# Layer 1's attention: DVE adds two of a head's four pair-sum tiles, and TensorE makes three products with ones a head instead of four

## The reference, cut to what matters

```python
q, k, v = (qkv[:, :, i].transpose(0, 2, 1, 3) for i in range(3))
attn = softmax(einsum('bhqd,bhkd->bhqk', q, k) * hd ** (-0.5), axis=-1)
o = einsum('bhqk,bhkd->bhqd', attn, v).transpose(0, 2, 1, 3).reshape(B, T, D)
```

## Time and profile before

| | |
|---|---|
| Time, median of 3 runs | 3868.43 us (3863.33 to 3868.81) |
| The profiled execution's own time | 3865.6 us |
| Its span | 3863.7 us |
| PE busy | 3588.0 us, 93% of the span |
| DVE busy | 2666.8 us, 69% |
| ACT busy | 2306.9 us, 60% |
| POOL busy | 1921.6 us, 50% |
| Mean granted clock of TensorE | 0.968 |

### The profile page before, as it was taken

The page is one execution under the profiler, slowest core; times in us unless marked ns, Lnnn a source line. Parts: engine busy times, 40 slices in busy tenths (PEclk is TensorE's granted clock), DMA queues, the critical chain, the costliest instruction groups (busy, mean ns, idle before and its releaser), DMA issues. The chain is left out here.

```text
span 3863.7 us, 68702 instructions
## 1 busy us (share of the span) xinstructions
PE 3588.0 (93%) x25924; PEld 2519.3 (65%) x25924; DVE 2666.8 (69%) x4271; ACT 2306.9 (60%) x4011; POOL 1921.6 (50%) x2187
## 2 busy tenths in 40 slices
PE   8997999999999989899999986889999999995999
PEld 7885777767777767777778863446666666652555
DVE  4335888888888866667753327867777777755987
ACT  2225888888888855333333326745555555554988
POOL 1003555555555533444444436646666666663554
PEclk9998999999999999999999998979999999997999
DMA  5546333333323139334431116853334333314221
GB/s 187 186 162 164 64 70 64 70 64 69 62 59 64 40 131 338 104 107 155 148 104 44 50 55 234 313 106 73 64 76 81 66 70 79 74 32 137 83 77 50
DMA packets 284776, 403.16 MB, mean 104 GB/s; under 512 B 89704, under 2 KB 146540, under 8 KB 283930
## 3 DMA queue, kind: packets, MB, share of 16 engines
q1 hardware_dynamic: 284448, 398.78, 37.3%
HBM read 248.95 MB, written 148.93 MB: 103 GB/s over the span
## 5 line engine op out<-in xcount | busy, mean ns | idle before, releaser
L634 POOL TENSOR_SCALAR biastile<-dist,ascale 128x1024 f32<-128x1024 f32 x512 | 574.9, 1123 | 489.4 <-DVE mn L588 476.2
L796 ACT ACTIVATE PT<-st 128x512 f32<-128x512 f32 x1024 | 544.9, 606 | 419.1 <-PE st L730 415.3
L810 DVE TENSOR_REDUCE mn<-s 128x1 f32<-128x1024 f32 x512 | 596.4, 1216 | 273.7 <-PE s L720 273.7
L873 POOL TENSOR_TENSOR two<-PT 128x1024 f32<-128x1024 f32 x256 | 603.5, 2377 | 305.0 <-ACT PT L796 304.9
L588 DVE CUSTOM_DVE_ANT_0 Sn<-sp,biastile 128x1024 f32<-128x1024 f32 x512 | 621.9, 1215 | 78.5 <-PE pt L521 46.7
L559 ACT ACTIVATE Sn<-Sn,mn 128x1024 f32<-128x1024 f32 x512 | 586.9, 1146 | 18.9 <-DVE mn L588 18.8
L521 PEld LDWEIGHTS pt<-ident,Sn 128*128 128x128 f32 x4096 | 454.9, 141 | 177.5 <-issue 150.9
L521 PE MATMUL pt<-ident,Sn 128*128 128x128 f32 x4096 | 546.9, 277 | 22.1 <-DVE og L601 22.1
L549 ACT ACTIVATE PT<-pt 128x512 f32<-128x512 f32 x576 | 337.6, 598 | 136.3 <-PE pt L521 126.3
L730 PE MATMUL st<-QS,KS 98*128 98x512 f32 x1024 | 376.4, 425 | 1.3 <-ACT PT L796 1.2
L720 PE MATMUL s<-KS,QS 96*128 96x512 f32 x1024 | 353.7, 428 | 25.3 <-DMA KS<-s_khi 23.6
(11 more groups left out here) (257 smaller groups left out, 6503.2 us busy)
## 6 DMA issues: line engine op xcount, KB each, us to landing
QS<-s_qhi SPq DMA_DIRECT2D x128, 256.0 KB, 5.1
KS<-s_khi SPq DMA_DIRECT2D x128, 256.0 KB, 6.9
KS<-s_klo SPq DMA_DIRECT2D x64, 256.0 KB, 6.2
QS<-s_qlo SPq DMA_DIRECT2D x64, 256.0 KB, 6.8
Vp<-s_v SPq DMA_DIRECT2D x64, 256.0 KB, 7.7
s_o<-og SPq DMA_DIRECT2D x32, 512.0 KB, 4.0
xA<-in_x SPq DMA_DIRECT2D x8, 1024.0 KB, 5.9
s_qhi<-qstage SPq DMA_DIRECT2D x32, 256.0 KB, 2.0
```

The costliest lines, as they stand in the source:

```text
L634: nc.gpsimd.tensor_scalar(bt[s % 2][:], dist[:, t, :], K.ascale[:, n % H:n % H + 1], 1.0, ALU.mult, ALU.mult).then_inc(*s_bias.up())
L796: nc.scalar.activation(pT[n % 2][:, kb, g * BLK:(g + 1) * BLK], pst_r.at["st", u, g][:], ACT.Exp, scale=-1.0).then_inc(*s_exp.up())
L810: nc.vector.tensor_reduce(mn[n % 2][:, t:t + 1], ps_r.at[u][:], AX.X, ALU.min).then_inc(*s_min.up())
L873: nc.gpsimd.tensor_tensor(two[m % 6][:], pT[n % 2][:, 2 * k, :], pT[n % 2][:, 2 * k + 1, :], ALU.add).then_inc(*s_two.up())
```

## The change

DVE adds the first two pair sums of a head, k = 0 and k = 1, in place into the buffer of k = 1. It does so in step 2n + 6, after the four minima and the copy `mr`, and signals `s_four`. `total(n)` now waits once for all four pair sums, makes the products of k = 2 and k = 3, waits for `s_four`, and makes the product of the tile that DVE has added. It signals `s_sum` once a head instead of four times, and the waits on it count heads.

```diff
+        def add_four(n):
+            m = n * LT // 2
+            dve.wait_ge(s_two, m + 2)
+            nc.vector.tensor_tensor(two[(m + 1) % 6][:], two[m % 6][:], two[(m + 1) % 6][:], ALU.add).then_inc(*s_four.up())
```

```diff
-        def total(m):
-            n, k = divmod(m, LT // 2)
-            pe.wait_ge(s_two, m + 1)
-            for g in range(4):
-                op = nc.tensor.matmul(po[g * HD:(g + 1) * HD, QW:2 * QW], K.ones[:, 0:HD], two[m % 6][:, g * QW:(g + 1) * QW],
-                                      start=k == 0, stop=k == LT // 2 - 1)
+        def total(n):
+            pe.wait_ge(s_two, (n + 1) * LT // 2)
+            for k in (2, 3, 1):
+                if k == 1:
+                    pe.wait_ge(s_four, n + 1)
+                for g in range(4):
+                    op = nc.tensor.matmul(po[g * HD:(g + 1) * HD, QW:2 * QW], K.ones[:, 0:HD],
+                                          two[(n * LT // 2 + k) % 6][:, g * QW:(g + 1) * QW], start=k == 2, stop=k == 1)
             op.then_inc(*s_sum.up())
```

```diff
@@ vector_program, after take_minima
+                n, odd = divmod(w - 6, 2)
+                if not odd and 0 <= n < N_HEADS:
+                    add_four(n)
@@ take_output
-            dve.wait_ge(s_sum, (n + 1) * LT // 2)
+            dve.wait_ge(s_sum, n + 1)
@@ add_pair
             if m >= 6:
-                pool.wait_ge(s_sum, m - 5)
+                pool.wait_ge(s_sum, (m - 6) // (LT // 2) + 1)
```

More of the change, by code:

```diff
@@ L666, in stage_attention1 @@
         s_row = [S.sem() for _ in range(2)]
-        s_ov, s_turn, s_rec, s_out = (S.sem() for _ in range(4))
+        s_ov, s_turn, s_rec, s_out, s_four = (S.sem() for _ in range(5))
         def load_pair(p):
@@ L786, in tensor_program @@
                 if not odd and 0 <= n < N_HEADS:
-                    for i in range(LT // 2):
-                        total(n * LT // 2 + i)
+                    total(n)
         def exponential(u, g):
```

## The result

The changed kernel takes 4008.76 us (median of 4 runs, 4005.15 to 4011.61) where the kernel before takes 3866.47 us (4 runs). The ratio is 1.0366, with a 95% interval from 1.0352 to 1.0379: slower by 142 us. The profiled execution took 4010.51 us, against 3865.6 before: 144.9 us more, and it is this difference that the traces have to explain.

The account below looks back on a forecast made before the run. PE was taken to bound layer 1's attention, with no spare time. Onto 3865.6 us came +93.3 (61 heads at +1.55, last three -1.3) and +21 for the clock: 3980 us, range 3950 to 4008.

Parts of the forecast that it names:

- PE sets the pace of the stage, one to one: Layer 1's attention: PE has no spare time, so a microsecond off or onto the end of `total` changes the head equally.
- The product, 0.43 us a head: In `total`, one of four products with ones goes: 0.43 us less a head, 27.7 us less over 64 heads.
- DVE arrives 0.36 us after the start of POOL's second sum and is held to its end: Even step: `add_four` reads two SBUF inputs, waits for POOL's sum and ends 1.08 us after it, at 3023.03.
- +1.55 us a head for the hold: PE's third product in `total` waits for DVE, so the next step starts 1.55 us later: 61 heads, +94.6 us.
- The last three heads gain 0.43 each, 1.3 together: Without minima ahead of DVE's addition, the last three heads gain up to 0.43 us each; taken as -1.3 us.
- The clock, +21 us for one head in four: After PE's gap of about 1.9 us the clock falls in one head in four: 15 x 1.4 = +21 us.
- the rival with falls in most heads: PE's clock falls after the gap in most heads, 61 x 1.4 us or more: 4044 us and up, chance 0.06.
- The range, 3950 to 4008: Whole kernel: from 1.50 us a head without clock falls to falls in every second head, with a little room.
- DVE in front of POOL: Rival: DVE's addition is not held or precedes POOL's second sum; 3848 us, at best 3838, chance 0.10.
- no change: Rival: PE would have waited anyway, or DVE is held only a part; 3868 us, chance 0.03.

Follow-up runs that it names:

- the product alone: Changed kernel without DVE's addition and the wait for it, pair sum k = 0 left out of the sums: 3839.39 us, ratio 0.9929 to the kernel before.

## Why the prediction was right, and where its size was off

- *PE sets the pace of the stage, one to one.* Right: the product alone gave 26.2 us of the 27.7 worked out, and a repeated product in the gap cost nothing.
- *The product, 0.43 us a head.* Right: 14.70 to 14.27 us.
- *DVE arrives 0.36 us after the start of POOL's second sum and is held to its end.* Right. It arrives 0.29 to 0.37 us after it (3007.71 against 3007.41 in the head shown), in the 54th head 0.65 us, and ends 1.08 or 1.09 us after POOL, as worked out, in all of the first 61 heads. The trace of before had only operations of half the length; the step from them to this one, on which all hangs, holds. The average of 1.60 us for the four POOL sums in the earlier trace rows hid that the first took 1.29 us and the three behind it 1.73 or 1.74, with a DVE operation between each two: DVE's first ended 0.55 us after POOL's first, the same hold as in the `xb` row, and POOL's next sum was held in its turn. The exclusive lock of the Trainium skill, SBUF — State Buffer, § Who interferes with whom, is what the runs show: 3136 ns with two SBUF inputs, 1197 with one, and with the order turned round it is POOL's sum that is held.
- *+1.55 us a head for the hold.* 1.50 was measured (16.20 against 14.70); the 0.05 for the weight load that no longer runs ahead did not show. 61 x 0.05 = 3 us too much.
- *The last three heads gain 0.43 each, 1.3 together.* They gained 0.5 together. DVE's operation took 1909 ns in the first of them and 1214 in the last two, and PE waited for it in none. But in the last head POOL's last pair sum was the one that was held, and `total`, which now asks for all four pair sums ahead of its first product, waited 0.60 us for it. The prediction had put that wait at nothing; in the other heads it was.
- *The clock, +21 us for one head in four.* This is the mis-sized term. The mechanism was right, the count was not: 46 falls instead of 15, each 1.17 us instead of 1.4, 54 us instead of 21. I took few falls on the ground that the matmuls around this gap are denser than around the gaps of the earlier trace rows that were followed by one. But the gap here, 1.72 us by the records, is longer than each of those four, and it was known to be (I had worked out 1.9 between the products): by length alone, all four rows lay on the side of fewer falls. And one of the two rows with a fall is weaker than it was taken for: the clock was already down at 1539.9, ahead of the product at 1540.36, in a stretch where PE had three gaps (0.97, 0.64 and 1.64 us) within 5 us. What happened is the rival with falls in most heads, which had 0.06 and a price of 1.4 us for each of 61 heads, 4044 us; with the measured hold, count and price it is 4010.
- *The range, 3950 to 4008.* Its upper end came from falls in every second head, and the median of 4008.76 lies 0.8 us above it. That it came so close is partly luck: three times as many falls, each cheaper than assumed, and a hold 0.05 us shorter. The range should have reached to falls in all heads.
- *The rivals.* DVE in front of POOL exists, but in the first 61 heads only when it is put there, about 1.3 us earlier (3840 us); 0.2 us earlier is not enough (4009 us). Nothing speaks for no change.

Whether the clock falls follows a rhythm of three heads with and one without, 46 and 15 of the 61, with a shift now and then. The length of the gap doesn't decide between them: it is 1.65 to 1.73 us in the heads with a fall and 1.70 to 1.73 in those without, except the 54th (1.38 us, no fall). The fall begins some 0.3 us earlier in the head from one to the next (4.9, 4.6, 4.3 us behind the copy `mr`), and then comes the head without one. So the time at which a gap comes seems to matter too. Why is open, and it was not tried.

## What to carry to other kernels

Before work is moved to DVE with two SBUF inputs, look at what POOL does in that very microsecond, and at who waits for the result: a hold that nobody waits for is free, and a change of place by one instruction can turn 142 us lost into 25 gained. Price a wait on a busy PE twice, once for its length and once for the clock behind it. And where an engine has idle time, its place in the step matters as much as its amount. In step 2n + 4 DVE had 3.2 us idle in a row and POOL 3.4. DVE's began 2.0 us before the pair sum was there (3869 us), POOL's right behind it (3839 us).

## What the runs showed of the hardware that I had not expected

- A gap on PE of 1.7 us in each head, in a stage that is busy otherwise, was followed by 3.4 us at half clock in 46 of 61 heads; one of 1.3 us in the same place, behind one product more, made no head longer. The half clock costs 1.17 us each time, not 1.7; the lines are below.
- Work whose result is thrown away made the kernel faster: one repeated product a head (0.43 us of PE's time) gave 50 us.
- A weight load may wait 0.24 us for its semaphore without its matmuls coming later.

For the price of the half clock, the two odd steps shown above can be laid side by side. From the start of the fourth to the start of the twelfth of their score products it takes 2.05 us at full clock (3012.30 to 3014.35) and 3.37 at half (3028.50 to 3031.87): 1.32 us more, and not twice as long. The rest of the scores gives 0.14 back. At full clock PE's weight loads have small waits in this place:

```profile
3013.38 0.19 PEld L730 LDWEIGHTS st<-QS,KS 98*128 98x128 f32 x1 [0.19 <-ACT PT L797]
3013.78 0.30 PEld L720 LDWEIGHTS s<-KS,QS 96*128 96x128 f32 x2 [0.21 <-DVE mn L811]
...
3014.63 0.19 PEld L730 LDWEIGHTS st<-QS,KS 98*128 98x128 f32 x1 [0.30 <-ACT PT L797]
```

At half clock there are none from 3028.50 to 3031.87. That fits a price under 1.7 us; it was not tried by a run of its own.
